# Cross-attention and a frequency-domain layer on one core: ScalarE casts a normalised context ahead of four exponentials, and four chunks' bias additions move behind a small multiplication on GpSimd

## The reference

```python
def attention(x, ctx, mask):                 # 16 heads of 32
    q, k, v = layernorm(x) @ wq + bq, ctx @ wk + bk, ctx @ wv + bv
    score = einsum('bhqd,bhkd->bhqk', q, k) / sqrt(32) * mask
    score = where(score == 0, -1e9, score)
    context = einsum('bhqk,bhkd->bhqd', softmax(score), v)
    return context @ wo + bo
x = x + attention(x, ctx, mask)
x = x + real(ifft(fft(layernorm(x)) @ w)) + bias
```

## Time and profile before

| | |
|---|---|
| median of 3 runs | 456.96 us (456.81 to 457.02) |
| time of the profiled execution | 456.98 us |
| its span, first to last instruction | 455.2 us |
| granted TensorE clock | 1.000 |
| busy: PE, DVE, ACT, POOL | 433.3, 403.5, 368.3, 353.0 us |

### The profile page before, as it was taken

How to read it: one execution, slowest core, us unless ns; L and a number is a source line. 1 busy time by engine, 2 the same in 40 slices (tenths; PEclk the granted TensorE clock), 3 DMA queues, 4 the chain that set the end, 5 groups by cost and what they waited for, 6 DMA issues and landing times.

```text
span 455.2 us, 10923 instructions
## 1 busy us (share of the span) xinstructions
PE 433.3 (95%) x3510; PEld 298.5 (66%) x3510; DVE 403.5 (89%) x538; ACT 368.3 (81%) x1342; POOL 353.0 (78%) x476
## 2 busy tenths in 40 slices
PE   6989897998999999999999999999999999989997
PEld 5777676777566676666676666666766665555444
DVE  3797699889999999999999999999999899999353
ACT  3358597789998989998989899899989899999620
POOL 6588844685879989798989898989899877755763
PEclk9999999999999999999999999999999999999999
DMA  8996662332426455564555445546443424341244
GB/s 287 389 376 183 234 199 70 93 92 60 107 72 153 109 156 115 141 133 125 117 153 117 132 87 138 128 123 153 108 104 66 109 69 115 55 92 24 71 110 122
DMA packets 85287, 60.15 MB, mean 132 GB/s; under 512 B 40142, under 2 KB 72814, under 8 KB 84719
## 3 DMA queue, kind: packets, MB, share of 16 engines
q1 hardware_dynamic: 84508, 59.29, 48.4%
q10 hardware_dynamic: 722, 0.17, 0.2%
HBM read 29.33 MB, written 8.39 MB: 83 GB/s over the span
## 4 chain that ended last, share of the span: by engine, by line
PE 58%; DVE 14%; POOL 10%; issue 8%; ACT 7%; DMA 1%; ACTq 1%; POOLq 0%; DVEq 0%
PE bank L454 24%; PE bank L459 15%; PE bank L611 7%; ACT zs L714 5%; PE bank L625 4%; DVE zs L904 4%; PE scores L599 3%; DVE zs L897 3%; PE bank L560 2%; POOL cl L1146 2%; POOL rzb L1140 2%; POOL xs L1093 2%; ACT pt L723 1%; PE bank L541 1%; DMA bqb<-in_bq 1%
## 5 line engine op out<-in xcount | busy, mean ns | idle before, releaser
L714 ACT ACTIVATE zs<-zs,nbias 128x128 f32<-128x128 f32 x512 | 199.5, 395 | 18.1 <-POOL nbias L1133 17.3
L714 ACT ACTIVATION_READ_ACCUMULATOR zs<-zs,nbias 128x1 f32 x512 | 98.4, 192 | 0.0
L904 DVE SCALAR_TENSOR_TENSOR zs<-zs 128x1024 f32<-128x1024 f32 x64 | 89.7, 1401 | 1.2
L909 DVE TENSOR_REDUCE nmin<-zs 128x8 f32<-128x1024 f32 x64 | 78.1, 1220 | 2.2
L897 DVE TENSOR_TENSOR zs<-scores,ms 128x1024 f32<-128x1024 f32 x64 | 78.1, 1220 | 1.0 <-issue 0.6
L723 ACT COPY pt<-bank 128x512 f32<-128x512 f32 x128 | 67.8, 580 | 13.5 <-PE bank L611 13.4
L611 PE MATMUL bank<-ident,zs 128*128 128x128 f32 x512 | 66.8, 273 | 1.9 <-ACT zs L714 1.9
L459 PE MATMUL bank<-xth,wqh 128*128 128x256 f16 x224 | 61.2, 273 | 1.3 <-DVE ql L869 1.3
L1093 POOL TENSOR_TENSOR xs<-xs,bob 128x512 f32<-128x512 f32 (+1 forms) x41 | 42.9, 1049 | 25.0 <-DVE zs L904 21.9
L459 PE MATMUL bank<-xtl,wqh 128*128 128x256 f16 x224 | 61.1, 273 | 0.0
L459 PE MATMUL bank<-xth,wql 128*128 128x256 f16 x224 | 61.1, 273 | 0.0
(11 more groups left out here) (126 smaller groups left out, 929.2 us busy)
## 6 DMA issues: line engine op xcount, KB each, us to landing
xs<-in_x SPq DMA_DIRECT2D x16, 512.0 KB, 4.5
xtr<-in_xt SPq DMA_DIRECT2D x16, 512.0 KB, 4.5
out<-x SPq DMA_DIRECT2D x31, 256.0 KB, 2.5
qs<-qh SPq DMA_DIRECT2D x120, 64.0 KB
lp<-in_lparts SPq DMA_DIRECT2D x4, 1024.0 KB, 8.3
qs<-ql SPq DMA_DIRECT2D x60, 64.0 KB
ms<-in_mask SPq DMA_DIRECT2D x16, 128.0 KB, 2.6
wqs<-in_wq SPq DMA_DIRECT2D x2, 512.0 KB, 6.9
```

The costliest lines, as they stand in the source:

```text
L714: last = act.activation(z, z, ACT.Exp, bias=nbias[:, s % 4, i:i + 1], scale=-NEG, accum_out=zsum[:, s % 4, i:i + 1])
L904: dve.scalar_tensor_tensor(out=z, in0=z, scalar=0.0, in1=z, op0=ALU.is_equal, op1=ALU.subtract).then_inc(eq_done, 1)
L909: dve.tensor_reduce(nmin[:, s % 4, :], zs[:, s % NZ].rearrange("p t h k -> p (t h) k"), AX.X, ALU.min).then_inc(mn_done, 1)
```

## The change

Two calls are written at another place of the loop. On ScalarE ctx_hi of the odd slots stands ahead of the second half of the exponentials and no longer behind it. On GpSimd the eight calls of add_bo for chunks 12 to 15 stand behind the slot's bias and no longer ahead of it; in odd slots they are thus between bias and ctx_lo. No instruction is added or removed.

```diff
@@ ScalarE
                 if 0 <= v - 2 < NS:
                     copy_pt(v - 2, 0)
                     copy_pt(v - 2, 1)
+                if v % 2 == 1 and 0 <= v - 5 < NS:
+                    ctx_hi((v - 5) // 2)
...
                 if 2 <= v - 1 < NS:
                     exps(v - 1, 1)
-                if v % 2 == 1 and 0 <= v - 5 < NS:
-                    ctx_hi((v - 5) // 2)
@@ GpSimd
-                for a in range(3, NC):
+                for a in range(3, 12):
                     if bo_slot(a) == v:
                         add_bo(a, 0)
-                    if bo_slot(a) + 1 == v and a >= 12:
-                        add_bo(a, 1)
                 if 0 <= v < NS:
                     bias(v)
+                for a in range(12, NC):
+                    if bo_slot(a) == v:
+                        add_bo(a, 0)
+                    if bo_slot(a) + 1 == v:
+                        add_bo(a, 1)
                 if v % 2 == 1 and 0 <= v - 5 < NS:
                     ctx_lo((v - 5) // 2)
```

## The result

| | before | after |
|---|---|---|
| median | 456.98 us (456.81 to 457.10, 6 runs) | 460.64 us (459.75 to 462.22, 6 runs) |
| ratio | | 1.0087, interval 1.0068 to 1.0107 |
| profiled execution, its span | 456.98, 455.2 us | 462.10, 460.3 us |
| granted TensorE clock in it | 1.000 | 0.996 |

The change costs 3.7 us, twice what the prediction says, and 0.24 us more than its range allows. The six runs fall into two groups: four with clock 1.000 (459.75, 460.42, 460.59 and 460.70, middle 460.5) and two with clock 0.996 (462.10 and 462.22). The profiled execution is one of the two, so its trace holds 1.5 us that the median lacks. Of the experiments' runs, one each of mild and keep55 (643 and 564 us, with a mean granted clock of 0.66 and 0.76) is left out; mild's is its profiled one, so mild has no trace at full clock.

The account below looks back on a forecast made before the run. TensorE was taken to bound 200 to 366 us and VectorE the tail to 421 us. The sum 0.40 + 0.12 + 0.6 + 0.9 - 0.1 = 1.9 us on 456.98 gave 458.9 us, range 457.4 to 460.4.

Parts of the forecast that it names:

- Slot 5, +0.40: ScalarE's early cast waits for VectorE's cn ahead of ready exponentials, so qh and ql come 0.40 us later.
- Slot 11, +0.12: The early cast waits for cn, so mh and VectorE's L888, which waited for it, come 0.12 us later.
- I leave this out of the sum and keep it for the range: Slot 11: if GpSimd's cl starts ahead of VectorE's L888, L888 ends 1.1 us later; not in the sum.
- All other casts, 0: Other early casts cost nothing: cn is there in time or ScalarE's pauses cover it, and TensorE's work hides later exponentials.
- The cast cannot give this back: Slot 55: cl waited 0.23 us for ch, but with the addition ahead of it no longer waits, so no gain.
- Slots 55 and 56, +0.6: Slot 55's addition now delays cl, so WO of chunk 12 starts 1.0 us later and VectorE's L876 loses 0.6.
- Slots 54 and 58, +0.9: GpSimd's add_bf meets VectorE's L904 in both slots; one taken as held and one not, +0.9 us, bounds +0.1 to +1.6.
- some 0.3: Slot 54, if VectorE's L904 starts first: GpSimd's late work then costs some 0.3 us in slot 55.
- Slot 60, -0.1: The earlier cast removes cl's wait and L876's 0.57 us wait, but x1nl lengthens L904 by 0.5: net -0.1 us.
- held in both slots: Rival: add_bf leads L904 in slots 54 and 58, +1.6, 459.6 us; 460.7 with cl ahead in slot 11; chance 0.3.
- Hidden: Rival: slot 5's delay is absorbed before 77.58 us and VectorE wins both add_bf meetings: 457.7 or 457.0 us; chance 0.17.
- faster: Rival: the early cast shortens TensorE's three waits for cl, 2.1 us together, against slot 5's 0.40: 455.3 us; chance 0.08.

Follow-up runs that it names:

- mild: Kernel before with ScalarE's cast early only from slot 13 on and GpSimd's additions behind the bias only in slots 54, 56, 58 and 60: 457.59 us, ratio 1.0008.
- keep55: Changed kernel with slot 55's addition alone back at its old place ahead of the bias: 459.95 us, ratio 1.0063.
- wait_slot11: Changed kernel, with GpSimd waiting in slot 11 for VectorE's L888 before it starts cl: 460.46 us, ratio 1.0081.
- add_slot55: Kernel before with slot 55's addition alone moved behind its bias: 458.50 us, ratio 1.0029.
- adds_only: Kernel before with only GpSimd's additions moved, ScalarE's cast at its old place: 459.26 us, ratio 1.0049.
- fill_wait: Changed kernel with 14 more TensorE products just ahead of WO of chunk 12, filling its wait for cl: 460.68 us, ratio 1.0080.
- wait_54_58: Changed kernel, with GpSimd waiting in slots 53 and 57 for the next slot's L904 before it starts add_bf: 459.86 us, ratio 1.0060.
- cast_only: Kernel before with only ScalarE's cast moved, GpSimd's additions at their old place: 458.15 us, ratio 1.0022.
- add_slot53: Kernel before with slot 53's addition alone moved behind its bias: 458.45 us, ratio 1.0030.
- late_wait: Kernel before with the cast early only in slots 55 and 59, and GpSimd's x1nl of slot 59 waiting for slot 60's L904: 456.43 us, ratio 0.9987.
- long_wait: Kernel before, with GpSimd waiting in slot 55 for the end of slot 56's VectorE scaling before it starts cl: 460.93 us, ratio 1.0087.
- adds_even: Kernel before with the additions behind the bias in slots 54, 56, 58 and 60 alone, no cast moved: 457.62 us, ratio 1.0016.

## Why the prediction was wrong

At full clock the kernel costs 3.5 to 3.6 us and the prediction says 1.9. Of the 1.7 that are missing 1.0 lies in slot 11 and 0.7 in slots 54, 58 and 59; without the two runs at 0.996 the middle would be 460.5, still above the range.

- **Slot 5, +0.40:** right, +0.33, by the chain that it gives. It did go through to the end.
- **Slot 11, +0.12: this step failed.** The mechanism was named, with its price (1.1), and then "I leave this out of the sum and keep it for the range". The working gave both starts as 113.73. The earlier order, L888 first, has no better claim than the other in such a tie, and the range stopped below the case. It measured 1.11, and wait_slot11 gives 1.0 of it back by the order alone.
- **All other casts, 0:** right between slots 13 and 53. The cast of slot 55 brings 0.25 in slot 56 when the additions stay put, which "The cast cannot give this back" covers only for the changed kernel, where it is right: the addition eats it (in keep55 it appears, -0.26).
- **Slots 55 and 56, +0.6:** right, 0.60 in add_slot55, 0.61 in adds_only and fill_wait. TensorE's wait was 1.6 to 2.3 in the traces, forecast 1.6. What it lacks is that this wait can bring the clock down for some 3.4 us, 1.6 us more in 5 of 16 runs. No row of before shows an idle TensorE of that length behind 366 us, nor a clock below 1.00 there; ahead of it its trace has idle stretches of 1.69 us from 30.64 and 1.71 from 106.09, with the clock at 1.00 in both.
- **Slots 54 and 58, +0.9: mis-sized.** "I take one slot held and one not" is a mean over two cases and a likely value of neither: both have the same sequence of calls, so both leads should come out alike. Both were held, by 0.02 us: 0.59 + 0.72, with 0.29 in slot 59, 1.60 in all, which is the bound that the prediction gives. Its other branch was too cheap as well: with VectorE first by force (wait_54_58) slot 55 pays 0.62 and not "some 0.3".
- **Slot 60, -0.1:** right in size and parts, -0.10 in after, -0.11 or -0.12 in the others.
- **The rivals:** *held in both slots*, with cl ahead of L888, stood at 460.7; the runs at full clock have 460.5 and the shifts give 460.6. The forecast's share belonged there. *Hidden* fails at slot 5 and the meetings, *faster* at cl of slot 55, by its own test: cl starts 1.42 behind nbias (382.17 against 380.75) and not 0.46 as in the earlier trace rows.

The back and forth of some 0.3 us in slots 34 to 37 is one more such meeting, far from every edit. Before, in slot 34:

```profile
249.93 1.23 DVE L904 SCALAR_TENSOR_TENSOR zs<-zs 128x1024 f32<-128x1024 f32 x1
249.95 1.67 POOL L1140 COPY rzb<-rz 128x512 f32<-128x512 f32 x1
```

After, both start at 251.41; rzb takes 0.61 and L904 1.70. L904 is held in the same way in cast_only, add_slot53, late_wait, long_wait and wait_slot11, and these six are the only traces with this shift, which leaves 0.1 behind. add_slot53, long_wait and the kernel before have the same instructions up to slot 53, and in add_slot53 rzb is recorded 0.03 after L904 (249.97 and 249.94) and still comes first. So the same work can fall either way here, for reasons that no trace shows.

## What to carry to other kernels

Work that fills an idle time on GpSimd is not free to move, even where that engine is idle for more than a quarter of the time, as in this tail (39.2 of 55 us busy): what matters is which of GpSimd's and VectorE's large calls starts first each time they meet, and that should be listed for every slot behind the move, since one late call brings the next meeting. Slots 54 and 58, with equal sequences, had equal outcomes, but slot 34 fell differently in kernels that were equal up to it; a tie of a few hundredths belongs in the sum at its dear side or as a case with half the chance, not left out. Where a moved call lengthens TensorE's idle stretch, ask what its clock does next, and read the clock of each run beside its time. A waiting call placed ahead of ready work should be moved only in the slots where its input is already there.

## What the runs showed of the hardware

- A lead of 0.02 us is enough: add_bf at 371.61 held L904 of 371.63 for 1.1. Below that the recorded starts do not tell who is held: cl at 114.08 held L888 of 114.09 for 1.01 us, in cast_only cl at 114.00 held L888 of 113.99, and in slot 34 rzb at 249.97 held L904 of 249.94 in add_slot53, while at 249.95 it was held by L904 of 249.93 before. The Trainium skill ("SBUF — State Buffer", section "SBUF: two separate sides") says that who starts first has the shared ports for the whole instruction; it names no least lead. For L904 and those of GpSimd's calls of 128x512 that start more than 0.03 us ahead of it or behind it, all traces agree.
- Not for the smallest: rstd2's L1103 (128x1, 0.57) at 386.78 was 0.04 ahead of L904 at 386.82, which took its plain 1.23. A call of 128x128 does hold: L1126's two parts, at 195.53 with 0.83 before, ended 0.26 after L904's start at 196.10, and L904 took 1.34. In adds_even its first part ended too soon for that to show (L904 1.22), and the second was held: 1.72 for both instead of 0.83.
- TensorE's granted clock went to 0.50 (1.2 GHz) near the end of an idle stretch of 1.85 us in the profiled run of the changed kernel (0.3 us before it), of 3.3 in that of long_wait (0.1 after it) and of 1.63 in that of wait_54_58 (0.5 after it), and was back at 1.00 some 3.4 us later each time; these times are worked out from the mean clock of stretches of 1 or 2 us, as above. All five runs of long_wait have the mean clock of 0.996 that goes with it. Behind 1.86 us in wait_slot11's profiled run and 2.26 in adds_only's it did not fall.
